# One run of score matmuls per group, over six PSUM banks that the projections share

## What is computed

```python
h = maximum(layernorm(x, axis=-1), 0.0)              # x: 64 graphs x 128 nodes x 384
q, k, v = heads(h @ Wq + bq), heads(h @ Wk + bk), heads(h @ Wv + bv)   # 6 heads of 64
scores = einsum('bhqd,bhkd->bhqk', q, k) / sqrt(64)
probs = softmax(scores + where(adj, 0.0, -9e15)[:, None], axis=-1)
ctx = einsum('bhqk,bhkd->bhqd', probs, v)            # heads joined again to 384
out = x + ctx @ Wf + bf
```

## Time and profile before

| | |
|---|---|
| runs | 469.63, 470.87, 470.64 us; median 470.64 us |
| profiled execution | span 468.2 us from the first to the last instruction; the profile gives no other time of its own for it |
| TensorE | 459.1 us busy (98%), granted clock 1.000 |
| VectorE, ScalarE, GpSimd | 365.0 us (78%), 361.6 us (77%), 303.1 us (65%) |
| first matmul of the first projection | 12.45 us after the start |
| last matmul starts | 464.84 us |
| chain that ended last | TensorE 88%, VectorE 4%, DMA 3%, ScalarE 2% |

### The profile page before, as it was taken

The page is one execution under the profiler, slowest core; times in us unless marked ns, Lnnn a source line. Parts: engine busy times, 40 slices in busy tenths (PEclk is TensorE's granted clock), DMA queues, the critical chain, the costliest instruction groups (busy, mean ns, idle before and its releaser), DMA issues.

```text
span 468.2 us, 12877 instructions
## 1 busy us (share of the span) xinstructions
PE 459.1 (98%) x4457; PEld 272.9 (58%) x4457; DVE 365.0 (78%) x742; ACT 361.6 (77%) x816; POOL 303.1 (65%) x308
## 2 busy tenths in 40 slices
PE   6999999999999999999999999999999999999986
PEld 2755656566575665646556575655656565555654
DVE  6989889849988695877869687687877957796855
ACT  3889999865987778877788787688877879687670
POOL 3378578683876765666857577368577648564574
PEclk9999999999999999999999999999999999999999
DMA  8156789879889796986959586969997787788797
GB/s 302 65 121 131 151 130 192 204 141 199 202 141 234 120 212 134 198 194 128 226 111 229 124 177 133 183 146 156 199 182 146 177 170 157 182 139 149 136 158 233
DMA packets 219615, 78.56 MB, mean 168 GB/s; under 512 B 199472, under 2 KB 219568, under 8 KB 219568
## 3 DMA queue, kind: packets, MB, share of 16 engines
q1 hardware_dynamic: 209200, 65.63, 71.5%
q10 hardware_dynamic: 10368, 12.33, 9.9%
HBM read 16.19 MB, written 12.58 MB: 61 GB/s over the span
## 4 chain that ended last, share of the span: by engine, by line
PE 88%; DVE 4%; DMA 3%; ACT 2%; SPq 1%; POOL 1%; issue 1%; ACTq 0%
PE ps_proj L1013 25%; PE ps_proj L1015 24%; PE ps_proj L1014 24%; PE ps_scores L1078 7%; PE ps_ctx L1013 2%; PE ps_ctx L1014 2%; PE ps_ctx L1015 2%; DMA ct_parts<-ctx_parts 1%; DMA pt_parts<-probs_parts 1%; DVE stats L822 1%; SPq L577 1%; ACT probs L757 1%; DMA x_sb<-in_x 1%; DVE w_rows L926 1%; ACT h_pairs L730 1%
## 5 line engine op out<-in xcount | busy, mean ns | idle before, releaser
L657 POOL TENSOR_TENSOR probs_parts<-probs,probs_parts 128x768 f16<-128x768 f32 x64 | 105.2, 1648 | 39.9 <-ACT probs_parts L772 39.8
L757 ACT ACTIVATE probs<-masked,neg_max 128x128 f32<-128x128 f32 x384 | 118.2, 389 | 14.4 <-DVE neg_max L885 8.2
L1015 PE MATMUL ps_proj<-ht_parts,w_lo 128*128 128x512 f16 (+1 forms) x309 | 109.6, 360 | 0.0
L1014 PE MATMUL ps_proj<-ht_parts,w_hi 128*128 128x512 f16 (+1 forms) x309 | 109.6, 360 | 0.0
L1013 PE MATMUL ps_proj<-ht_parts,w_hi 128*128 128x512 f16 (+1 forms) x309 | 109.6, 360 | 0.0
L857 DVE SCALAR_TENSOR_TENSOR qkt_lo<-ps_proj,bias_qk,qkt_hi 128x512 f16<-128x512 f32 x94 | 68.5, 742 | 27.8 <-ACT qkt_hi L741 27.8
L741 ACT ACTIVATE qkt_hi<-ps_proj,bias_qk 128x512 f16<-128x512 f32 x94 | 62.7, 679 | 34.2 <-PE ps_proj L1015 33.9
L663 POOL TENSOR_TENSOR ctx_parts<-ctx_sb,ctx_parts 128x384 f16<-128x384 f32 x62 | 56.7, 918 | 49.9 <-ACT ctx_parts L778 49.9
L876 DVE SCALAR_TENSOR_TENSOR masked<-ps_scores,score_unscale,mask 128x384 f32<-128x384 f32 x128 | 72.0, 609 | 10.3 <-PE ps_scores L1078 9.5
L642 POOL TENSOR_TENSOR h_pairs<-h_sb,h_pairs 128x384 f16<-128x384 f32 x60 | 54.3, 916 | 37.1 <-ACT h_sb L732 36.9
L652 POOL TENSOR_TENSOR x_bf<-x_sb,b_out 128x384 f32<-128x384 f32 x64 | 63.1, 1001 | 9.6 <-DVE y_sb L908 8.1
(11 more groups left out here) (113 smaller groups left out, 916.6 us busy)
## 6 DMA issues: line engine op xcount, KB each, us to landing
x_sb<-in_x ACTq DMA_DIRECT2D x56, 192.0 KB, 3.0
y<-y_sb SPq DMA_DIRECT2D x56, 192.0 KB, 2.5
x_sb<-in_x SPq DMA_DIRECT2D x8, 192.0 KB, 5.1
y<-x_bf SPq DMA_DIRECT2D x8, 192.0 KB, 3.3
pt_parts<-probs_parts SPq DMA_TRANSPOSE x64, 4.0
ct_parts<-ctx_parts SPq DMA_TRANSPOSE x62, 2.8
adj_sb<-in_adj ACTq DMA_DIRECT2D x14, 64.0 KB, 3.6
w_raw<-in_Wk SPq DMA_DIRECT2D x1, 576.0 KB, 5.1
```

Of the source, the lines that this page charges most:

```text
L657: nc.gpsimd.tensor_tensor(probs_parts[b][:, 1, :], probs[b % 2][:], probs_parts[b][:, 0, :], ALU.subtract).then_inc(probs_split, 1)
L757: last = nc.scalar.activation(probs[b % 2][:, u * N:(u + 1) * N], masked[b % 2][:, u, :], ACT.Exp, bias=neg_max[b % 2][:, u:u + 1])
L1014: nc.tensor.matmul(to, a_hi, b_lo, start=False, stop=False)
L1015: return nc.tensor.matmul(to, a_lo, b_hi, start=False, stop=last)
```

## The change

- **PSUM**: one tensor of eight banks. A table gives a bank to each use. Banks 0 to 5 hold the scores of all four graphs of a group and, between the score runs, `project_qk`; banks 6 and 7 take, in turn, `project_v`, `project_out` and `weigh_values`. Some items of groups 0 to 2 and 13 to 15 have banks of their own (`OWN_BANK`). `free_bank` waits for the reader of what the bank held before.
- **Scores**: `scores(g, part, i)` now has three parts of 24 matmuls, each filling two banks; the wait for masks between the pairs and the semaphore `lower_done` are gone.
- **SBUF**: `masked` and `neg_max` have four buffers, and the exponentials write in place; `mask_scores` waits for `probs_lo` of the same graph one group earlier, and `exponentials` waits for the row maximum only.
- **Order**: `TURNS` and `OWN_TURNS` are new numbers for all stages. The reductions of the weights (`reduce_rows`) stay on VectorE.

The arithmetic is the same. Of the score runs three are split by other work on TensorE: in group 1 (`weigh_values` before the third part), group 2 (two `project_v`, two `project_out`) and group 15 (one `project_out`).

```diff
-PROJ_BANKS = 4
-SCORE_PAIRS = ((4, 2), (5, 3), (0, 4), (1, 5), (2, 0), (3, 1))
+BANKS = 8
+SCORE_BANKS = 6
+ROW_SUM_BANK = 7
 TURNS = {
-    "scores": (5609, 7814), "mask_scores": (6121, 7156, 8482, 9829), "largest_score": (6841, 7995, 9320, 10570),
+    "scores": (0, 10, 20), "project_v": (30, 60, 80, 90), "project_out": (10130, 10140, 10190, 20040),
+    "project_qk": (-9950, -9930, -9890, -9840, -9830, -9820), "weigh_values": (150, 200, 10100, 10120),
...
+BANK = {
+    "project_qk": (0, 3, 1, 4, 2, 5), "project_v": (6, 7, 6, 7), "project_out": (6, 7, 6, 7),
+    "weigh_values": (6, 7, 6, 7),
+}
...
-        masked = [sb(f"masked{n}", [P, HEADS, N]) for n in range(2)]
-        neg_max = [sb(f"neg_max{n}", [P, HEADS]) for n in range(2)]
-        probs = [sb(f"probs{n}", [P, HEADS * N]) for n in range(2)]
+        masked = [sb(f"masked{n}", [P, HEADS, N]) for n in range(B)]
+        neg_max = [sb(f"neg_max{n}", [P, HEADS]) for n in range(B)]
+        probs = [masked[n][:].rearrange("p u n -> p (u n)") for n in range(B)]
...
             def exponentials(g, b, i):
                 act.wait_ge(max_ready, nth(B, g, b, i))
-                if g >= 1 or b >= 2:
-                    act.wait_ge(probs_split, nth(B, g, b - 2, i))
...
             def mask_scores(g, b, i):
-                dve.wait_ge(scores_ready, nth(2, g, b // 2, i))
+                dve.wait_ge(scores_ready, nth(SCORE_PARTS, g, LAST_PART[b], i))
...
-                if g >= 1 or b >= 2:
-                    dve.wait_ge(probs_ready, nth(B, g, b - 2, i))
+                if g >= 1:
+                    dve.wait_ge(probs_split, nth(B, g - 1, b, i))
...
             def free_bank(stage, group, item, i):
-                before = bank_before(stage, group, item)
-                if before is not None:
-                    was, of, at = before
+                for was, of, at in USES_BEFORE[stage, group, item]:
...
+                    if was == "weigh_values":
+                        pe.wait_ge(ctx_normalized, nth(B, of, at, i))
+                    if was == "scores":
+                        pe.wait_ge(scores_masked, nth(B, of, at + 1, i))
...
-            def scores(g, pair, i):
-                if pair == 0:
+            def scores(g, part, i):
+                if part == 0:
                     pe.wait_ge(qk_split, nth(QK, g, QK - 1, i))
-                if g == 0 and pair == 0:
-                    pe.wait_ge(v_split, 1)
-                if g >= 1 or pair >= 1:
-                    pe.wait_ge(scores_masked, nth(B, g, 2 * pair - 1, i))
+                free_bank("scores", g, part, i)
...
-                for n, heads in enumerate(SCORE_PAIRS):
-                    if n == MIDDLE_BY_UPPER:
-                        pe.wait_ge(lower_done, nth(2, g, pair, i))
+                for n in range(SCORE_SLOTS):
+                    b, k = divmod(SCORE_SLOTS * part + n, K)
```

More of the change, by code:

```diff
@@ L44 @@
 TURNS = {
[L45 to L50, removed]
@@ L66 @@
     0: {
[L67 to L72, removed]
@@ L164 @@
+    9: {
+        "weigh_values": (150, 200, 10110, 10130), "project_out": (10140, 10150, 10190, 10250),
+        "normalize_ctx": (260, 10010, 10160, 10170), "finish": (10180, 10200, 10290, 10350),
+        "ctx_hi": (300, 10090, 10130, 10170), "ctx_lo": (160, 10040, 10070, 10090),
+        "transpose_ctx": (10010, 10020, 10060, 10070), "store": (10130, 10170, 10190, 10230),
     },
     10: {
-        "project_qk": (0, 10, 40, 50, 60, 70), "qk_hi": (0, 30, 60, 100, 110, 120),
-        "qk_lo": (70, 90, 110, 120, 140, 150), "project_v": (80, 110, 120, 130), "values_hi": (160, 180, 200, 210),
@@ L168 @@
-        "values_lo": (220, 240, 250, 260), "residual": (0, 10, 40, 130), "scores": (100, 150),
-        "mask_scores": (160, 170, 270, 360), "largest_score": (180, 290, 300, 380),
-        "exponentials": (220, 240, 270, 350), "probs_hi": (230, 280, 340, 380), "probs_lo": (140, 160, 190, 200),
-        "transpose_probs": (90, 140, 150, 230), "weigh_values": (240, 290, 370, 410),
-        "normalize_ctx": (430, 520, 650, 690), "ctx_hi": (400, 560, 610, 660), "ctx_lo": (220, 320, 340, 370),
-        "transpose_ctx": (180, 250, 290, 310), "project_out": (360, 460, 470, 510), "finish": (600, 810, 830, 860),
@@ L174 @@
-        "store": (370, 380, 390, 440),
+        "project_v": (30, 60, 70, 80), "weigh_values": (160, 200, 310, 360), "project_out": (330, 390, 400, 460),
+        "values_lo": (70, 90, 100, 130), "mask_scores": (0, 30, 60, 190), "largest_score": (20, 40, 80, 240),
+        "normalize_ctx": (230, 300, 460, 550), "finish": (540, 620, 630, 730), "values_hi": (20, 60, 80, 100),
+        "exponentials": (10, 40, 210, 290), "probs_hi": (30, 70, 260, 330), "ctx_hi": (240, 250, 410, 500),
+        "probs_lo": (20, 30, 160, 180), "ctx_lo": (150, 220, 230, 290), "transpose_probs": (30, 40, 110, 120),
@@ new lines @@
+        "values_hi": (-19430, -19300, -19290, -19200), "exponentials": (-19410, -19370, -19360, -19250),
+        "load": (-29800, -29740, -20000, -19950), "probs_hi": (-19400, -19320, -19310, -19220),
+        "ctx_hi": (-19160, -19040, -19030, -18860), "normed_lo": (-19940, -19920, -19900, -19890),
+        "residual": (-19730, -19700, -19690, -19640), "probs_lo": (-19660, -19620, -19580, -19520),
+        "ctx_lo": (-19510, -19460, -19450, -19400), "transpose_probs": (-19680, -19670, -19620, -19580),
@@ new lines @@
+        "normalize_ctx": (-38520, -38480, -38390, -38300), "finish": (-38360, -38280, -38270, -38210),
+        "qk_hi": (-39000, -38990, -38980, -38890, -38840, -38830), "normalize": (-39190, -39180, -39170, -39120),
+        "values_hi": (-38800, -38790, -38740, -38540), "load_mask": (-39010,),
+        "exponentials": (-38780, -38750, -38720, -38670), "load": (-39380, -39350, -39340, -39330),
+        "probs_hi": (-38760, -38730, -38710, -38640), "ctx_hi": (-38600, -38570, -38550, -38470),
+        "inverse_deviation": (-39610,), "normed_lo": (-39560, -39550, -39540, -39530),
```

477 lines of the change are left out of this document (249 added, 228 removed).

## The result

| | before | changed |
|---|---|---|
| median | 470.60 us (469.63 to 470.87) | 472.73 us (472.29 to 473.19) |
| ratio | 1 | 1.0052, 95% interval 1.0038 to 1.0066 |
| profiled execution | 468.2 us | 471.2 us |
| last matmul starts | 464.84 us | 467.81 us |

The kernel became 0.5% slower, by 2.1 us; forecast were 1.7 us less. The page of the changed kernel begins like that of before: TensorE is full and its clock at the upper level throughout.

The account below looks back on a forecast made before the run. TensorE's work, 98% busy and without holes except around score runs, was taken as the bound. From a 468.2 us span, -2.5 + 1.1 + 0.5 + 0.7 - 1.5 = -1.7 gives 466.5, plus 2.4 to the median: 468.9 us, range 466.2 to 472.8.

Parts of the forecast that it names:

- Part 1: Ends of score runs on TensorE: 19 runs instead of 32, 0.19 us each, saving 2.5 us.
- Part 2: Banks 6 and 7 in the loop: `weigh_values` 2 waits 0.15 to 0.2 us in each of six groups, +1.1 us.
- other places in the loop, by the same durations: Other loop links, walked with the same durations: all covered, by 0.1 and 0.3 us, the first mask most thinly; no cost.
- Its own sign of being wrong: Loop: the prediction is wrong if TensorE's waits there exceed 0.25 us per group.
- Part 3: Single places: group 1's mask +0.5 us, groups 10 to 15 together +0.7 us; nothing new at the start.
- The 0 for the start: Start of the kernel: same pieces in almost the same order, its one 0.2 us wait for `v_lo` stays, 0 us added.
- Part 4: Tail: TensorE's starts 1.1 us late in place of 2.6, the long `v_lo` wait gone, saving 1.5 us.
- 0.4 us for the output side: Tail: 0.4 us lost on the output side, besides 0.7 us for the last transpose of probabilities.
- the prediction's last sign of being wrong: Tail: the prediction is wrong if TensorE still waits 2 us there.
- The two banks become the bound: Rival, chance 0.16: VectorE late at the first mask delays each group's chain, 0.4 us of stall per group, 472.7 us.
- Everything fits: Rival, chance 0.17: no stall arises in the body, only the savings at score-run ends and tail remain, 466.6 us.
- The clock drops: Rival, chance 0.02: small stalls bring one of 40 slices to the 1.2 GHz clock, adding 11.7 us, 480.6 us.

Follow-up runs that it names:

- e4: Changed kernel with the merge of score runs undone in seven groups (4 to 10); 473.99 us, 1.0087 of the kernel before.
- e1: Changed kernel with VectorE's `shift` in the loop behind the second `normalize_ctx` instead of before it; 469.89 us, 0.9997 of the kernel before.
- e12: Changed kernel with ScalarE's third and fourth `values_hi` of a loop group behind the third `probs_hi`; 478.39 us, 1.0179 of the kernel before.
- e13: Changed kernel, no order altered; in the loop GpSimd waits for `shift` before the `probs_lo` behind its rstd; 470.29 us, 1.0009 of the kernel before.
- e6: Changed kernel with ScalarE's `normalize` of graphs 2 and 3 of group 1 ahead of three weight splits; 473.17 us, 1.0061 of the kernel before.
- e5: Changed kernel with ScalarE's `ctx_hi` of graph 1 of the last group ahead of `values_hi` 3; 472.87 us, 1.0061 of the kernel before.
- e9: e5 with a third `ct_parts` buffer, used by graph 1 of the last group alone; 471.67 us, 1.0048 of the kernel before.
- e14: e11 with the edit of e13 in place of that of e1; 467.94 us, 0.9964 of the kernel before.
- e11: Changed kernel with the edits of e1, e9 and e10 together; 467.93 us, 0.9967 of the kernel before.
- e10: e6 with the last `mask_scores` of group 0 ahead of `shift` of group 2 on VectorE; 472.44 us, 1.0050 of the kernel before.
- e7: Changed kernel with the edits of e1, e5 and e6 together; 469.79 us, 0.9994 of the kernel before.

## Why the prediction was wrong

**Part 1 was right.** There are 13 runs fewer, 2.5 us, on the path; e4 puts 0.2 us apiece back. The other places ate it: with the loop's stalls alone mended (e1) the kernel takes the time of the kernel before, as the ledger has it (2.9 less 2.85), and only with start and tail mended too is it 0.3% faster.

**Part 2 had the right link and missed its neighbour.** The walk said that `values_hi` 2 starts 12.3 us after the first score matmul and that TensorE may go on at 13.45. In the trace the run of the first loop group starts at 131.18, `values_hi` 2 at 143.45 and `weigh_values` 2 at 144.59: 12.27 and 13.41. TensorE got there at 13.36, not 13.3, so the hole was 0.05 us where 0.15 to 0.2 stood; in six groups it came to 0.4 us for the 1.1 of the sum. A reserve of 0.06 us cannot be told from none by such a walk, and e12 shows that a delay beyond it is paid in full. What failed is the sentence "other places in the loop, by the same durations": it goes through masks, splits and the first mask, but not through `normalize_ctx` 3, which `project_out` 1 awaits over bank 7. In front of it stands `shift`, which waits for GpSimd. The sum had nothing for this link; it cost 2.85 us, 0.39 to 0.56 in each group, and score runs of successive groups are 28.20 to 28.41 us apart where the prediction expected 27.97. Its own sign of being wrong, more than 0.25 us per group, had come. With 0.16 us for `shift` the link holds with some 0.3 us to spare: in e13 the context ends at 149.57, TensorE wants it at 150.04 (all is 0.95 us later there than in the changed kernel), and from the one to the other 0.14 us pass in the changed kernel. It is the length of 1.60 us that made a stall of it. That length stood in the trace of before too, as its longest record (1502 ns); the prediction took VectorE's durations from one group only the earlier trace rows.

The Trainium skill has the rule, on the page "SBUF — State Buffer", section "Who interferes with whom": a VectorE instruction with two inputs in SBUF contends with a GpSimd instruction that reads SBUF, and the one that comes second is blocked until the first has ended. `shift` reads moments and rstd from SBUF, and the runs agree: 1.60 us with the overlap, 0.16 without it in e13. The next `ctx_sb` of VectorE, which has one input in PSUM, takes its usual 0.56 us at 148.94 although GpSimd works from 148.74 to 149.65. By that rule the places to look at are VectorE's instructions with two tensors in SBUF as inputs, next to a new order on GpSimd.

**Part 3** was right for group 1 (0.44 for 0.5) and too careful for groups 10 to 15 (0.3 for 0.7). The 0 for the start, for "the same pieces in almost the same order", was wrong by 2.0 us. The second half of ScalarE's normalization of group 1 had moved behind two splits of weights, 3.65 us later, and the prediction did not check what had covered it in the old order. e6 takes it ahead again and the wait is gone. That wait is 1.7 of the 2.0 us, some 1.2 of them by the slower landing; the rest lies in small holes around the first score run.

**Part 4.** The long wait for v_lo went, as forecast, and the transpose of probabilities costs 0.56 for 0.7. The "0.4 us for the output side" was 1.49 us, so that the tail still lost 2.05 us for the 1.1 of the sum, which was the prediction's last sign of being wrong. The missed price is a buffer: the second `ct_parts` is free only after `project_out` 3 of group 14, which the new order puts late. e5 shows that it was not ScalarE's order, and e9 and e14, in which the wait is gone, that it was the buffer; e11 shows that a late landing can bring 0.85 us of it back.

**The step from span to median.** The sum was added to a span of 468.2 us, and 2.4 us were carried over to the median. One and the same execution of the changed kernel has 473.13 us and a span of 471.2, 1.9 us apart, and those of the kernel before beside the experiments are 1.7 to 1.8 us apart. The other 0.6 us thus come, as far as the records tell, from taking the span of one execution and the median of others. They hide part of the error: by the medians the forecast is 3.8 us off, by the ledger 4.6.

**The rivals.** "The two banks become the bound" gave the measured number (472.7) and the right sign, for a wrong reason, which is luck, and so is it that the measured time lies just inside the stated range: it had VectorE late at the first mask, and there TensorE never waits in the loop. Nor does its price carry over. Its point of 0.25 us per group stands for 14 groups, 3.5 us in all; the stalls stood in six, 2.85 us, and without the 2.0 us of the start the kernel would have been 0.9 us slower in place of 2.9. "Everything fits" was refuted by six stalls; its 466.6 had also left out the 1.2 us of part 3. "The clock drops" was refuted by a mean granted clock of 1.000 in all four runs.

## What to carry to other kernels

When an order is packed so that TensorE has no slack, walk every link of the period that frees a bank or a buffer, not only the one that looks tightest, and for each ask what stands ahead of the freeing instruction in its engine's list and on which other engine that waits. A tiny instruction is no tiny cost: look at its longest record in the trace, not only its shortest, and at what the neighbour runs at that moment. A gain at one place is worth only as much as the reserve of the next link: e6 and e10 gave 0.8 and 1.0 us for stalls of 1.4 and 2.1.

## What the runs showed of the hardware

VectorE's 128x4 instruction on two SBUF operands (`shift`) took 0.15 to 0.17 us alone, 0.95 beside a GpSimd addition of 1.00 us, 1.60 beside one of 1.64 us and 1.27 where that one had begun 0.39 us earlier: each time it ended 0.01 to 0.03 us after GpSimd, and the whole time is recorded as busy. In e13 the waiting `probs_lo` of GpSimd starts 0.08 us after it.

Executions of one kernel differ in the mean granted clock. In e11 nine at a clock of 1.000 have a median of 467.88 us, three at 0.996 have 470.57. The profile of e6 is one of the latter, and the stretches of it (us, then busy times, with the granted clock before the DMA share) show where:

```profile
12.00:14.00 2.00, 1.91 (x17) 1.78 (x15) 2.00 (x5) 0.75 (x2) 0.00 (x0) 0.50 0.98 328
14.00:16.00 2.00, 2.00 (x32) 2.00 (x30) 1.97 (x6) 0.81 (x2) 0.00 (x0) 0.79 0.06 19
16.00:18.00 2.00, 2.00 (x42) 2.00 (x40) 1.58 (x7) 2.00 (x5) 0.00 (x0) 1.00 0.04 8
```

The clock stands at its lower level, 1.2 GHz, for some 3 us, after TensorE had waited 1.8 us for the first h. The same wait is in the profile of the changed kernel, whose clock stayed at 2.4 GHz, and the kernel before has executions at 0.996 too, though no wait for h in its profile is over 0.8 us. Why only some fall is open. Between the two kinds lie 0.9 (e7) to 2.7 us (e11) in the changed kernel's variants and 0.05 to 1.1 us in the kernel before. That is as much as anything studied here, so differences under 1 us were read from the traces between landmarks, not from medians.

Open also is why the four transposes at the start land after a median of 4.0 us where the kernel before had 2.7.
